# Two PSUM tensors in turn for the Q/K and QKV projection loops of a transformer kernel on eight cores

## What is computed

```python
def _L1_attn_ref(x, W_qkv, b_qkv, W_out, b_out, rel_emb_k, rel_emb_v):
    ...
    qkv = (x @ W_qkv + b_qkv).reshape(b, s, 3, H, hd)
    qkv = jnp.transpose(qkv, (2, 0, 3, 1, 4))
    q, k, v = (qkv[0], qkv[1], qkv[2])
    q = q / jnp.sqrt(jnp.asarray(hd, x.dtype))
    score = jnp.einsum('bhqd,bhkd->bhqk', q, k) + jnp.einsum('bhqd,qkd->bhqk', q, pe_k)
    attn = jax.nn.softmax(score, axis=-1)
    ...

def _layer(x, wqkv, qs, ksc, wo, lg, lb, w1, b1, w2, b2):
    b, n, _ = x.shape
    h = shift_token(x)
    qkv = h @ wqkv
    q, k, v = jnp.split(qkv, 3, axis=-1)
    ...
    x = x + o @ wo
    ...
    h = h @ w1 + b1
    a, g = jnp.split(h, 2, axis=-1)
    h = a * jax.nn.gelu(g, approximate=False)
    x = x + h @ w2 + b2
    return x
```

## Time and profile before

| | |
|---|---|
| time, median of 2 runs | 10321.15 us (10294.11 and 10348.18) |
| the profiled execution, its time | 10237.04 us |
| its span, slowest core (7) | 10235.5 us |
| spans of cores 0 to 7 | 10096.1, 10118.1, 10141.1, 10155.2, 10063.6, 10077.3, 10198.5, 10235.5 us |
| mean granted TensorE clock of the cores | 0.635 to 0.641 |
| busy share of the span | PE 51%, DVE 27%, ACT 16%, POOL 8% |
| Q/K loop of block 2 | starts at 1261.69 us on core 7, from 1255.9 to 1262.4 on the eight |
| QKV loops of block 3 on core 7 | start at 6300.38 and 8186.88 us |

### The profile page before, as it was taken

One profiled execution on the slowest core, in us unless ns is written; L12 is line 12 of the kernel. 1 busy time (PEld: TensorE's weight loads), 2 busy tenths in 40 slices (PEclk: granted clock), 3 DMA queues, 4 the chain that ended last, 5 costly groups with the idle time before them and its releaser, 6 DMA issues.

```text
span 10235.5 us, 60184 instructions; the slowest of 8 cores (10063.6 to 10235.5 us)
## 1 busy us (share of the span) xinstructions
PE 5252.5 (51%) x19111; PEld 2005.1 (20%) x19111; DVE 2728.8 (27%) x3977; ACT 1670.3 (16%) x3009; POOL 840.4 (8%) x813
## 2 busy tenths in 40 slices
PE   4352564555555555555555563233449743444894
PEld 2111121111112121111111121011114311111341
DVE  5756402000000000000000012633351135334314
ACT  2100011222222222222222200011101010111100
POOL 0000000000000000000000000211111112111010
PEclk7675795555555555555555576555569875556896
DMA  3000131111111111111111112000004310000331
GB/s 58 10 4 0 41 42 29 39 38 39 39 37 33 36 34 33 39 39 39 39 34 39 38 50 53 5 1 0 0 6 39 33 15 0 0 1 5 29 33 66
DMA packets 458424, 285.26 MB, mean 28 GB/s; under 512 B 307482, under 2 KB 403995, under 8 KB 454027
## 3 DMA queue, kind: packets, MB, share of 16 engines
q0 software_dynamic: 222240, 81.89, 7.0%
q1 hardware_dynamic: 180588, 120.34, 4.3%
q10 hardware_dynamic: 55296, 79.19, 2.1%
HBM read 227.39 MB, written 118.96 MB: 34 GB/s over the span
## 4 chain that ended last, share of the span: by engine, by line
PE 43%; DVE 18%; DMA 16%; ACT 12%; issue 6%; SPq 3%; DVEq 1%; POOL 1%; ACTq 1%; POOLq 0%; PEldq 0%; PEld 0%
PE pm L1143 5%; ACT xb L1138 5%; DMA sc_amax<-amaxc 5%; DMA sc_qre<-wm 4%; PE pm L1926 3%; PE pb L1947 3%; DMA wj<-sc_amax 3%; SPq L49 3%; DVE wm L972 2%; PE pm L1121 2%; PE pm L1436 2%; PE pb L1156 2%; PE pm L1992 2%; PE pb L1992 2%; PE pb L1740 2%
## 5 line engine op out<-in xcount | busy, mean ns | idle before, releaser
L972 DVE RECIPROCAL wm<-pm 1x512 f32<-1x512 f32 x64 | 214.5, 3352 | 3514.3 <-PE pm L968 3514.3
L1138 ACT ACTIVATE xb<-pm 128x512 bf16<-128x512 f32 x1024 | 611.4, 597 | 1968.2 <-PE pm L1131 1181.1
L1143 PE MATMUL pm<-xb,U 128*65 128x512 bf16 x576 | 342.5, 595 | 605.0 <-ACT xb L1138 605.0
L1705 DVE TENSOR_REDUCE amaxc<-pm 128x1 f32<-128x640 f32 (+4 forms) x256 | 181.8, 740 | 783.2 <-PE pm L1701 781.8
L49 POOL DMA_DIRECT2D wj<-sc_qre x128 | 70.5, 553 | 3721.8 <-PE pm L1126 2331.2
L1013 PE MATMUL pb<-wj 128*128 128x512 bf16 x256 | 139.7, 556 | 434.7 <-ACT wm L1020 398.9
L1751 ACT ACTIVATE xb<-pb 128x512 bf16<-128x512 f32 x448 | 243.3, 595 | 558.3 <-PE pb L1740 558.3
L1121 PE MATMUL pm<-qer,wj 128*128 128x512 bf16 (+4 forms) x576 | 308.1, 535 | 0.0
L1131 PE MATMUL pm<-wj 128*128 128x512 bf16 (+4 forms) x576 | 290.3, 504 | 0.0
L220 PE MATMUL pm<-xb,wj 128*128 128x512 bf16 x512 | 143.8, 451 | 280.8 <-ACT U L231 258.3
L1728 PE MATMUL pb<-wm,zbuf 1*65 1x512 bf16 x64 | 38.6, 603 | 448.2 <-DMA wj<-sc_amax 448.2
(11 more groups left out here) (435 smaller groups left out, 9433.1 us busy)
## 6 DMA issues: line engine op xcount, KB each, us to landing
sc_qre<-wm ACTq DMA_DIRECT2D x256, 256.0 KB, 2.0
xb<-sc_e SPq DMA_DIRECT2D x256, 128.0 KB, 2.3
wm<-l1f_w POOLq DMA_DIRECT2D x116, 256.0 KB, 4.3
sc_xspill<-xr SPq DMA_DIRECT2D x16, 1024.0 KB, 13.6
wm<-W_qkv POOLq DMA_DIRECT2D x48, 256.0 KB, 4.2
sc_e<-xb ACTq DMA_DIRECT2D x112, 96.0 KB, 2.0
sc_e<-xb SPq DMA_DIRECT2D x112, 96.0 KB, 1.9
xin<-x SPq DMA_DIRECT2D x16, 512.0 KB, 4.1
```

The lines of the kernel that those rows point to most:

```text
L972: p.op("vector", lambda q, c2=ctxp: q.reciprocal(out=srow[0:1, 0:512], in_=c2[64:65, 0:512]))
L1138: q.activation(out=o, in_=i_, func=AF.Exp), s_se)
L1143: q.matmul(o, l, r, start=st, stop=False), None)
```

## The change

In both loops the groups go to `pm` for even and to `pb` for odd output tiles, with one eviction token for each. PE waits before tile `dd` for the eviction of tile `dd - 2` in place of that of `dd - 1`, and the eviction reads the tensor that the group wrote. In block 2 a wait is added before the loop, since VectorE's copies of L715 to L720 read `pb`. The weight buffers and their loads are as they were; the waits behind the loops take the last eviction, as before.

```diff
     p.wait("tensor", s_xsp, s_xsp.n)
     p.wait("tensor", s_ve, tok_pvb)
-    evq_tok = 0
+    p.wait("tensor", s_ve, tok_pve)
+    evqb2 = [0, 0]
     for dd in range(16):
+        psq = pm if dd % 2 == 0 else pb
         p.wait("tensor", s_wq[dd % 2], 16 * (dd // 2 + 1))
-        if evq_tok:
-            p.wait("tensor", s_se, evq_tok)
+        if evqb2[dd % 2]:
+            p.wait("tensor", s_se, evqb2[dd % 2])
...
-                p.op("tensor", lambda q, o=pm[:, nb * 512:(nb + 1) * 512], l=lhsT, r=rhs,
+                p.op("tensor", lambda q, o=psq[:, nb * 512:(nb + 1) * 512], l=lhsT, r=rhs,
...
-                 i_=pm[:, nb * 512:(nb + 1) * 512], b=bqkvc[:, dd:dd + 1], s=sc:
+                 i_=psq[:, nb * 512:(nb + 1) * 512], b=bqkvc[:, dd:dd + 1], s=sc:
...
-        evq_tok = p.sems["s_se"].n
+        evqb2[dd % 2] = p.sems["s_se"].n
...
-    p.wait("tensor", s_se, evq_tok)
+    p.wait("tensor", s_se, p.sems["s_se"].n)
```

More of the change, by code:

```diff
@@ L1423, in build_block3 @@
         p.wait("tensor", s_ve, hsh_tok)
-        evq = 0
+        evqb = [0, 0]
         qkv_mm_last = 0
         for dd in range(12):
+            ps = pm if dd % 2 == 0 else pb
             p.wait("tensor", s_w3[dd % 2], (bq0 if dd % 2 == 0 else bq1) + 16 * (dd // 2 + 1))
-            if evq:
-                p.wait("tensor", s_se, evq)
+            if evqb[dd % 2]:
+                p.wait("tensor", s_se, evqb[dd % 2])
             for nb in range(NB):
                 for dt in range(NDT):
-                    p.op("tensor", lambda q, o=pm[:, nb * 512:(nb + 1) * 512],
+                    p.op("tensor", lambda q, o=ps[:, nb * 512:(nb + 1) * 512],
                          l=wqb[dd % 2][:, dt * 128:(dt + 1) * 128],
@@ L1442, in build_block3 @@
                 p.op("scalar", lambda q, o=QKV[dd][:, nb * 512:(nb + 1) * 512],
-                     i_=pm[:, nb * 512:(nb + 1) * 512]:
+                     i_=ps[:, nb * 512:(nb + 1) * 512]:
                      q.activation(out=o, in_=i_, func=AF.Copy),
                      s_se if nb == NB - 1 else None)
-            evq = p.sems["s_se"].n
+            evqb[dd % 2] = p.sems["s_se"].n
             if dd + 2 < 12:
@@ L1449, in build_block3 @@
                 load_wq3(dd + 2)
-        qkv_tok = evq
+        qkv_tok = p.sems["s_se"].n
         p.wait("gpsimd", s_tr, qkv_mm_last)
```

## The result

| | before | after |
|---|---|---|
| median of the slowest core, us | 10322.8 (42 executions) | 10192.9 (43) |
| lowest, highest | 10155.7, 10525.6 | 9997.5, 10386.5 |
| profiled execution, us | 10237.0 | 10184.5 |
| ratio of the times, 95% interval | | 0.977 [0.973, 0.981] |

The medians differ by 130 us (1.26%), the ratio says 2.3%, about 235 us. The forecast was 118 us. The ratio compares only the executions near each kernel's fastest, of the changed kernel four (9997 to 10100 us, mean 10034.0) and of the kernel before, as far as its list of times tells, 19 (10156 to 10308 us, mean 10269.9): 10034.0 / 10269.9 = 0.977. Why the two differ is the subject of most of what follows.

A forecast was written before the change was run, and what follows sets the result against it. PE and ScalarE taking turns on `pm` was taken as the bound in the changed loops. Net gains of 43.6 + 37.2 + 37.6 = 118.4 us, off the 10321.15 us median, gave 10202.8, stated as 10200, range 10100 to 10300.

The forecast's parts named there:

- Block 2's loop, 106.19 us from the first to the last start: Block 2's 16-tile loop: first to last group start falls from 156.31 to 106.19 us, a gain of 50.1 us.
- The added wait, 6.5 us: Before block 2's loop: PE waits for VectorE's copies that read `pb`, costing 6.5 us, with nothing hiding it.
- Block 3, 78.27 and 78.80 us: Block 3's loops, layers 0 and 1: first to last start; gains 37.2 and 37.6 us including the last groups.
- Weights cost nothing, ready at 4.9 of 6.9 us: Changed loops: each weight load lands within the one group that covers it, so its cost is zero.
- What follows waits for the loop: Behind the changed loops: a microsecond given up comes off the core's end, unless a later transfer catches it.
- Rival of the lower grant: Changed loops run at the lower granted clock, costing 59.5 us; gain 59 us, 10262 us; chance 0.15.
- The slower rival: Denser loops bring the lower grant into all cores' up- and down-projections, costing 196 us; 10458 us; chance 0.05.
- Rival of the weight load: Changed loops: the weight load becomes the bound, costing 48 us; gain 70 us, 10251 us; chance 0.08.
- How the numbers follow: Whole kernel: takes 118.4 us off the 10321.15 us median, giving 10202.8, with the spread in untouched stages; says 10200.
- the gain is not seen in the end: Block 3's attention loops: another run may put a slower core on top; gain about 0, 10321 us; chance 0.07.
- more than forecast: Block 3's attention loops: denser groups leave the slowest core in a luckier course; about 10110 us; chance 0.05.
- ratio: Whole kernel: the sum is 1.15%; chance 0.91 of within 2%, 0.07 of faster by more, 0.02 of slower.

The follow-up runs named there:

- e3: Changed kernel with VectorE's copies of pvE, which block 2's loop waits for, moved ahead of its three memsets: 10189.0 us, ratio 0.982.
- e5: Changed kernel, but POOL issues each weight load only after the tile's eviction, not its last matmul: 10287.6 us, single execution.
- e1: The change in block 2's loop alone, block 3 as in the kernel before: 10251.4 us, ratio 0.9975.
- e2: The change in block 3's two loops alone, block 2 as in the kernel before: 10232.0 us, ratio 0.995.
- e6: Changed kernel with block 3's row of maxima made on chip by four matmuls and a copy, replacing the `sc_amax` transfers: 9905.7 us, ratio 0.949.
- e7: Kernel before the change, with the same on-chip row of maxima replacing the `sc_amax` transfers: 10066.5 us, ratio 0.962.
- e8: The changed kernel again, unedited, beside the kernel before on a third chip: 10302.2 us against 10385.3, ratio 1.003.
- e9: Changed kernel with both the on-chip row of maxima and VectorE's copies of pvE ahead of its memsets: 9864.5 us, ratio 0.951.
- e4: Changed kernel, tensors still alternating, but PE waits for the eviction of the group just before: 10418.8 us against 10424.6, ratio 1.001.

## Why the prediction was wrong, point by point

- *Block 2's loop, 106.19 us from the first to the last start*: 1265.59 to 1372.06, 106.47. Right; the cold first group was 9.94 against 9.69.
- *The added wait, 6.5 us*: 6.75 us from L711's end, of which the kernel before had none to speak of (it started at once, 1261.69). Right within 0.3. VectorE does three memsets before the copies, not two (on core 7 before 1.76, 1.76 and 0.48 us); the time was taken from the copies' end, so the sum doesn't suffer. What would have been better is in e3: most of the wait was avoidable.
- *Block 3, 78.27 and 78.80 us*: 78.96 in layer 0 and 78.87 in layer 1, core 7. Right.
- *Weights cost nothing, ready at 4.9 of 6.9 us*: 5.0, no wait. Right, and e5 shows how near the edge is.
- *What follows waits for the loop*: right. e1 gives 40 for 43.6 in both heaps, e2 76 and 78 for 74.8; e6 against e7 gives 118 to 120 for 118.4 with the second course out of the way. The sum of 118.4 us stands.
- *Rival of the lower grant*: met, on one pair of cores in some loops, at up to 22 us in block 2's and 17 in block 3's; by the forecast's price a matmul they are 24 and 18, and it had all three loops. *The slower rival* had the lower grant in the projections of all cores, brought on by the denser loops: 98 us a layer. The grant is there, on pairs and up to that size (560 and 566 us in place of 467 in e8), but the kernel before has it too (535 and 538 us on cores 2 and 3 in the very trace that was read, 532 to 559 in e7), so nothing shows that the change brings it on. *Rival of the weight load*: no sign, but in e5, where it was made.
- *How the numbers follow*: here it failed. The step reads "the spread belongs to the stages that are not touched. Taken off the median it gives 10202.8". The first half is right; the second treats the spread as a band that both kernels have alike. The median came out 10 us below the 10202.8, but the measured ratio is 2.3% where the step had 1.15% and gave 0.07 to more than 2%. The runs showed in its place that the spread is no band round a median: pairs of cores fall into heaps 170 to 200 us apart, by the slow course in the attention and by lower grants in the projections, and the time is that of the worst pair. A comparison of slowest cores then reads the kernel's difference plus one of heaps. That the median came so near is luck as much as the sum: with the same two kernels it moved by 130 us in one comparison and by 83 in another. The same pair of kernels gave 0.977 and 1.003, medians -130 and -83, and heaps shifted by -91 and -88 within session 3, by -134 and -106 from session 1 to its own. Two rivals, "the gain is not seen in the end" (0.07) and "more than forecast" (0.05), were this mechanism; they were named with the right stage and their price (core 3's 90 us in rows 12), and given far too little for a spread of 172 us in the page's first line and a forecast of 118. Their mechanism was half right: no run shows that denser groups steer the course.
- The forecast's *ratio* term was mis-sized so: 118 us forecast, 236 in the ratio (10269.9 - 10034.0), of which the loops are 118 by e6 and e7. The other 118 are put down to heaps: four executions of the changed kernel without a slow pair, and 19 of the kernel before up to 10308 us, which mostly have one (in session 1, where the cores are on record, two of its 35 executions have none, and its upper heap is at 10279). That part is worked out, not shown by a run of its own.

Shown: the slow course hangs on the `sc_amax` transfers and the waits for them, since it is gone when they are (e6, e7, e9). Open: what sets a pair's course and a pair's grant (for the course the phase at which its two cores enter the loops is an idea only; cores that share a path for small writes and reads would show the exchanged 9 us and 4.5 us, but no run tests it). Open too: whether the change alters the share of slow pairs (shares of 0.40, 0.47 and 0.59 for before, 0.56 and 0.50 after, 0.31 to 0.46 for its variants, say nothing clear), and why e8's heaps shift by 27 to 30 us less than 118 where its lowest pair shifts by 115.

## What to carry to other kernels

Price a closed gap from a neighbouring loop of the same shape that already has the overlap: 6.905 us a group there was 6.91 here. Where the cores of one execution end further apart than the gain you forecast, find what they differ in before you turn a sum into a ratio, and compare heaps of cores rather than the slowest core. A small row that goes through DRAM inside a loop of dependent steps can cost more than its landing time: here the slow course of two neighbouring cores went with it, and four matmuls against the identity in its place were worth three times this change (e7's median is 358 us under before's). Where a stage is dense, look at each core's granted clock in it before putting a difference down to anything else.

## What was not expected of the hardware

- The `sc_amax` writes of 0.5 KB land in 5.9 to 6.8 us in the two profiles, and in 9.2 to 9.6 on one core of a slow pair, whose partner's 1 KB reads take 4.3 to 4.8 in place of 1.9 to 2.3; this exchanges between the partners from one execution to another.
- The lower grant comes by pairs of cores, not by dies: 0.81 on cores 0 and 1 and 0.95 on core 2 in the same 125 us of the same loop. In the projections it costs a pair up to 98 us a layer (565 us at 0.81 in place of 467 at 1.00), with either kernel.
- Chips differ by some 80 to 110 us for the same program: lower and upper heaps of before 10110 and 10279 on one, 10187 and 10391, 10194 and 10367 on two others. The traces put most of this into the attention part: in its good course a layer takes 1145 to 1177 us on the first chip, 1181 to 1217 (e4, e5) and 1186 to 1215 (e8) on the two others, and with `sc_amax` gone 1080 to 1092 on both of those. The transfers themselves are slower there: the writes take 7.4 us and the reads 2.3 on e5's core 2, where the changed kernel's core 2 had 6.7 and 2.0.
